# Low-part waits at the third product, and four operations moved in the order of a gated graph kernel

## The reference

```
def _L1_gnn_ref(input, in_matrix, out_matrix, ...):      # both matrices are adj
    def step(h, _):
        m_in = jnp.einsum('nm,bmd->bnd', in_matrix, h)
        m_out = jnp.einsum('nm,bmd->bnd', out_matrix, h)
        av = jnp.concatenate([m_in, m_out], axis=-1)
        u3 = h @ u3_w.T + u3_b
        z = jax.nn.sigmoid(av @ w3_w.T + w3_b + u3)
        r = jax.nn.sigmoid(av @ w4_w.T + w4_b + u3)
        hv = jnp.tanh(av @ w5_w.T + w5_b + (r * h @ u5_w.T + u5_b))
        return (1.0 - z) * h + z * hv, None
    h, _ = jax.lax.scan(step, input, None, length=5)
x = _layernorm(x + L0(x, adj))          # (adj x + x) W0 + b0, rows scaled to length 1
x = _layernorm(x + _L1_gnn_ref(x, adj, adj, ...))
x = _layernorm(x + L2(x, adj))          # D^-1/2 (adj + 1) D^-1/2 x W^T + b, D the row sums
x = _layernorm(x + L3(x, adj))          # softmax mix by a mask of adj, two weights
```

## Time and profile before

| | |
|---|---|
| median of 3 runs | 739.24 us |
| the profiled execution's own time | 740.75 us |
| its span, first to last instruction | 739.0 us |
| mean granted clock of PE | 0.995 |
| busy: PE, PE weight load, VectorE, ScalarE, GpSimd | 98%, 81%, 84%, 69%, 32% |
| slots 47 to 81, mean | 6.26 us |

### The profile page before, as it was taken

The page is one execution under the profiler, slowest core; times in us unless marked ns, Lnnn a source line. Parts: engine busy times, 40 slices in busy tenths (PEclk is TensorE's granted clock), DMA queues, the critical chain, the costliest instruction groups (busy, mean ns, idle before and its releaser), DMA issues.

```text
span 739.0 us, 11595 instructions
## 1 busy us (share of the span) xinstructions
PE 727.3 (98%) x3532; PEld 599.9 (81%) x3536; DVE 622.6 (84%) x1463; ACT 510.5 (69%) x1057; POOL 239.4 (32%) x368
## 2 busy tenths in 40 slices
PE   8999999999999989999999999999999999999996
PEld 7888787788887777777777777778888888889886
DVE  5899888999887878988888888878899999887775
ACT  4899878876666757766666666666687867863333
POOL 0878322312222312222222222220123257664433
PEclk9999999999999999999999999999999999999999
DMA  6600013334446463353333333330000000101112
GB/s 202 243 1 2 1 33 78 76 86 96 96 97 152 83 92 85 86 141 85 85 84 80 81 85 87 85 72 1 2 0 1 1 0 2 29 1 44 58 52 78
DMA packets 149661, 49.21 MB, mean 67 GB/s; under 512 B 134368, under 2 KB 135904, under 8 KB 149088
## 3 DMA queue, kind: packets, MB, share of 16 engines
q1 hardware_dynamic: 149072, 48.47, 27.2%
q10 hardware_dynamic: 528, 0.00, 0.0%
HBM read 25.11 MB, written 21.24 MB: 63 GB/s over the span
## 4 chain that ended last, share of the span: by engine, by line
PE 85%; ACT 6%; DVE 5%; DMA 3%; issue 1%; SPq 0%; POOL 0%; POOLq 0%; ACTq 0%; DVEq 0%
PE agg_ps L1161 14%; PE agg_ps L1163 13%; PE agg_ps L1162 13%; PE gate_ps L1075 7%; PE gate_ps L1077 7%; PE gate_ps L1076 7%; PE cand_ps L1075 5%; PE cand_ps L1076 4%; PE cand_ps L1077 4%; PE gate_ps L1082 3%; PE cand_ps L1082 3%; DMA state_blocks<-cand 2%; ACT feat L576 1%; PE turn_ps L1206 1%; ACT res L483 1%
## 5 line engine op out<-in xcount | busy, mean ns | idle before, releaser
L671 POOL TENSOR_TENSOR nat_lo<-nat_lo,nat_hi 128x512 fp32r<-128x512 f32 x61 | 80.5, 1320 | 293.7 <-ACT agg_hi L512 293.7
L1161 PE MATMUL agg_ps<-adj_hi,nat_hi 128*128 128x512 f32 x384 | 154.4, 402 | 0.0
L1163 PE MATMUL agg_ps<-adj_hi,nat_lo 128*128 128x512 f32 x384 | 150.4, 392 | 0.0
L1162 PE MATMUL agg_ps<-adj_lo,nat_hi 128*128 128x512 f32 x384 | 150.1, 391 | 0.0
L879 DVE TENSOR_TENSOR agg_lo<-agg_ps,agg_hi 128x512 fp32r<-128x512 f32 x80 | 55.0, 687 | 48.9 <-ACT agg_hi L512 48.9
L537 ACT ACTIVATE gate_r<-gate_ps,bias 128x512 f32<-128x512 f32 x80 | 55.2, 690 | 52.0 <-PE gate_ps L1077 52.0
L512 ACT ACTIVATE agg_hi<-agg_ps 128x512 fp32r<-128x512 f32 x80 | 48.2, 602 | 56.2 <-PE agg_ps L1163 56.2
L1163 PEld LDWEIGHTS agg_ps<-adj_hi,nat_lo 128*128 128x128 f32 x384 | 72.4, 188 | 15.9
L1162 PEld LDWEIGHTS agg_ps<-adj_lo,nat_hi 128*128 128x128 f32 x384 | 72.6, 189 | 14.2
L1161 PEld LDWEIGHTS agg_ps<-adj_hi,nat_hi 128*128 128x128 f32 x384 | 72.6, 189 | 13.8
L703 POOL TENSOR_SCALAR shift<-mean_var 128x4 f32<-128x4 f32 x62 | 24.0, 388 | 153.3 <-DVE mean_var L937 151.3
(11 more groups left out here) (207 smaller groups left out, 1751.7 us busy)
## 6 DMA issues: line engine op xcount, KB each, us to landing
state_blocks<-cand SPq DMA_DIRECT2D x61, 256.0 KB, 2.1
nat_lo<-state_blocks SPq DMA_DIRECT2D x244, 64.0 KB, 2.5
res<-in_x SPq DMA_DIRECT2D x16, 256.0 KB, 6.4
out<-res SPq DMA_DIRECT2D x16, 256.0 KB, 2.0
rows<-in_adj SPq DMA_DIRECT2D x4, 256.0 KB, 5.1
adj_hi<-eye_hi SPq DMA_DIRECT2D x1, 1024.0 KB, 9.8
adj_lo<-eye_lo SPq DMA_DIRECT2D x1, 1024.0 KB, 11.6
mix_rows<-mix SPq DMA_DIRECT2D x4, 256.0 KB, 2.8
```

Source lines behind the costliest of these rows:

```text
L671: pool.tensor_tensor(flat(nat_lo[:, u % B, :, :]), flat(nat_lo[:, u % B, :, :]).bitcast(F32), flat(nat_hi[:, u % B, :, :]).bitcast(F32), A ...
L1161: pe.matmul(ps, nat_hi[:, b, k, :], m_hi[:, k, :], start=(k == 0), stop=False)
L1162: pe.matmul(ps, nat_hi[:, b, k, :], m_lo[:, k, :], start=False, stop=False)
L1163: last = pe.matmul(ps, nat_lo[:, b, k, :], m_hi[:, k, :], start=False, stop=(k == T - 1))
```

## The change

The wait for the low part (feat_lo, agg_lo, reset_lo) moves from before a product's first matmul to before its third; the first waits for the high part. On VectorE the reset state's low part is computed before the state's add instead of after it. The row sums run one a slot in slots 40 to 43 instead of two; what follows from them moves: `WHOLE_AT` from 42 to 45, `L2_AT` from 48 to 52, row_d on GpSimd from slot 42 to 44, its transfer from slot 43 to 45, d_cols from slot 45 to 48. `SWAP_LAG` goes from 5 to 6.

```diff
--- before.py
+++ after.py
@@ -122,8 +122,8 @@
 LATE_AT = [at + 2 for at in CHOSEN_AT]
 VALUE_AT = [at + 2 for at in CHOSEN_AT]
 SUM_AT = VALUE_AT[-1] + 3
-WHOLE_AT = SUM_AT + 2
-L2_AT = WHOLE_AT + T + 2
+WHOLE_AT = SUM_AT + T + 1
+L2_AT = WHOLE_AT + T + 3
 assert L2_AT + T <= 4 * B
 
 DIAG_AT = LAST
@@ -163,7 +163,7 @@
 TURN_NO = {x: i for i, x in enumerate(TURNS)}
 
 
-SWAP_LAG = 5
+SWAP_LAG = 6
 Z_BEHIND = 0
 
 TURNED = [u for u in range(B, LAST) if u not in BY_DMA]
@@ -424,7 +424,7 @@
                     sp.wait_ge(const_made, consts)
                     sp.wait_ge(mix_stored, 16 * T)
                     sp.dma_start(diag[:, :], cells, allow_slow_non_contiguous=True).then_inc(diag_in, 16)
-                if s == SUM_AT + 5:
+                if s == WHOLE_AT + 3:
                     sp.wait_ge(d_stored, 16)
                     sp.wait_ge(turned, TURN_NO["value", T - 1] + 1)
                     sp.dma_start(d_cols[:, :], d_dram[0:1, :].to_broadcast([P, N])).then_inc(d_cols_in, 16)
@@ -595,11 +595,11 @@
                         own = slice(k * P, (k + 1) * P)
                         last = act.activation(adj_hi[:, k, own], turn_ps[n % 2][:, own], ACT.Copy)
                     last.then_inc(adj_hi_made, 1)
-                for k in range(2 * (s - SUM_AT), 2 * (s - SUM_AT) + 2):
-                    if 0 <= k < T:
-                        act.wait_ge(rows_again, 16)
-                        act.activation(chosen[:, k, :], later[:, k, :], ACT.Copy,
-                                       accum_out=row_sum[:, k:k + 1]).then_inc(row_sum_made, 1)
+                k = s - SUM_AT
+                if 0 <= k < T:
+                    act.wait_ge(rows_again, 16)
+                    act.activation(chosen[:, k, :], later[:, k, :], ACT.Copy,
+                                   accum_out=row_sum[:, k:k + 1]).then_inc(row_sum_made, 1)
                 if s in CHOSEN_AT:
                     k = CHOSEN_AT.index(s)
                     act.wait_ge(mask_made, T)
@@ -615,7 +615,7 @@
                         act.activation(w_all[:, W_L2, :], turn_ps[n % 2][:, cols:cols + D], ACT.Copy)
                     act.activation(w_hi[:, w, :], turn_ps[n % 2][:, 0:cols].rearrange("p (a d) -> p a d", d=D),
                                    ACT.Copy).then_inc(w_hi_made, 1)
-                if s == SUM_AT + 3:
+                if s == WHOLE_AT:
                     act.wait_ge(row_d_made, 1)
                     act.dma_start(d_dram[0].rearrange("(t p) -> p t", p=P), row_d[:, :],
                                  allow_slow_non_contiguous=True).then_inc(d_stored, 16)
@@ -705,7 +705,7 @@
                     pool.tensor_tensor(rstd[:, i % RING, :], r, half[:, :], ALU.pow).then_inc(rstd_made, 1)
                     pool.wait_ge(rstd_made, i + 1)
                     pool.tensor_tensor(back, back, rstd[:, i % RING, :], ALU.mult).then_inc(shift_made, 1)
-                if s == SUM_AT + 2:
+                if s == SUM_AT + T:
                     pool.wait_ge(row_sum_made, T)
                     link(pool.tensor_scalar(row_sum[:, :], row_sum[:, :], 1.0, None, ALU.add))
                     pool.tensor_tensor(row_d[:, :], row_sum[:, :], half[:, :], ALU.pow).then_inc(row_d_made, 1)
@@ -902,16 +902,16 @@
                     dve.wait_ge(feat_hi_made, s - B + 1)
                     dve.tensor_tensor(feat_lo[:, :], feat[:, s % B, :], feat_hi[:, :].bitcast(F32),
                                       ALU.subtract).then_inc(feat_lo_made, 1)
+                u = s - 1
+                if is_step(u):
+                    dve.wait_ge(reset_hi_made, u - B + 1)
+                    dve.tensor_tensor(reset_lo[:, :], gate_r[:, u % 2, :], reset_hi[:, :].bitcast(F32),
+                                      ALU.subtract).then_inc(reset_lo_made, 1)
                 u = s - 2
                 if is_step(u):
                     dve.wait_ge(move_made, u - B + 1)
                     dve.tensor_tensor(feat[:, u % B, :], feat[:, u % B, :], cand[:, u % 2, :],
                                       ALU.add).then_inc(state_made, 1)
-                u = s - 1
-                if is_step(u):
-                    dve.wait_ge(reset_hi_made, u - B + 1)
-                    dve.tensor_tensor(reset_lo[:, :], gate_r[:, u % 2, :], reset_hi[:, :].bitcast(F32),
-                                      ALU.subtract).then_inc(reset_lo_made, 1)
                 u = s - STATE_LAG
                 if is_inner(u) and u not in BY_DMA:
                     dve.wait_ge(state_hi_made, nth(TURNED, u))
@@ -1070,10 +1070,12 @@
             pe.wait_ge(eye_lo_made, T)
             first_sums(1, 2).then_inc(agg_done, 1)
 
-            def product(ps, w, hi, lo, start, stop):
+            def product(ps, w, hi, lo, start, stop, lo_made=None, count=0):
 
                 pe.matmul(ps, w_hi[:, w, :], hi, start=start, stop=False, skip_group_check=True)
                 pe.matmul(ps, w_lo[:, w, :], hi, start=False, stop=False, skip_group_check=True)
+                if lo_made is not None:
+                    pe.wait_ge(lo_made, count)
                 return pe.matmul(ps, w_hi[:, w, :], lo, start=False, stop=stop, skip_group_check=True)
 
             def by_rows(ps, m, w, stop):
@@ -1167,8 +1169,9 @@
                 u = s - 2
                 if is_step(u):
 
-                    pe.wait_ge(reset_lo_made, u - B + 1)
-                    product(cand_ps[u % 2][:, :], U_CAND, reset_hi[:, :], reset_lo[:, :], False, True).then_inc(cand_done, 1)
+                    pe.wait_ge(reset_hi_made, u - B + 1)
+                    product(cand_ps[u % 2][:, :], U_CAND, reset_hi[:, :], reset_lo[:, :], False, True,
+                            reset_lo_made, u - B + 1).then_inc(cand_done, 1)
                 u = s - 1
                 gate = gate_ps[u % 2][:, :]
                 parts = agg_hi[:, u % 2, :], agg_lo[:, u % 2, :]
@@ -1180,10 +1183,10 @@
                     if u == B:
                         pe.wait_ge(turn_read, reads(TURN_NO["weights", 1]))
 
-                    pe.wait_ge(feat_lo_made, u - B + 1)
-                    product(gate, U_GATE, feat_hi[:, :], feat_lo[:, :], True, False)
-                    pe.wait_ge(agg_lo_made, u - B + 1)
-                    product(gate, W_R, *parts, False, True).then_inc(gate_done, 1)
+                    pe.wait_ge(feat_hi_made, u - B + 1)
+                    product(gate, U_GATE, feat_hi[:, :], feat_lo[:, :], True, False, feat_lo_made, u - B + 1)
+                    pe.wait_ge(agg_hi_made, u + 1)
+                    product(gate, W_R, *parts, False, True, agg_lo_made, u - B + 1).then_inc(gate_done, 1)
                     if u >= B + 2:
                         candidate(u)
                 elif 0 <= u < UNITS:
```

## The result

The changed kernel takes 728.24 us (median of 4 runs, 728.07 to 729.18) against 739.12 us (4 runs, 737.57 to 740.31) of the kernel before: a ratio of 0.9857, 95% interval 0.9836 to 0.9877. The profiled execution's own time is 728.07 us with a span of 726.3. Forecast were 727.5 us, and 727.3 for the span. The two spans are 12.7 us apart.

The account below looks back on a forecast made before the run. PE, busy 727.3 of 739.0 us, bounds the kernel, so matmuls must come closer together. Gains of 9.1 (reset wait) and 2.6 (large stall) make 11.7, from the median of 739.24 to 727.5 us; range 725.4 to 732.2.

Parts of the forecast that it names:

- The reset wait: PE's first reset-state weight load waits for reset_lo; removing this gains 9.1 us over all slots, bounds 7.6 and 9.6.
- The second part of the loss: In ordinary slots, 0.10 us is lost at the wait and the rest of 0.14 while matmul spacing settles again.
- Slots 23 to 26: Loaded gate-step slots, two with 27 matmuls and two with 31, falling from 27.45 to 25.5 us, gain 1.9.
- The nine further slots: Slots 19, 31, 34, 37, 39, 40, 82, 89, 94: gain 0.14 us each, two some 0.15 larger, 1.5 together.
- slot 41: This slot of 7.30 us keeps its other stall and loses the reset one, gaining 0.3 us.
- both edits are needed in the loaded slots: In slot 24, reset_lo in the add's place ends at 125.26: too late for 125.08, in time for 125.53.
- a collision: VectorE's L899 took 1.80 us while GpSimd's first L671 ran; that L671 moves a slot, so this goes, within 1.9.
- The large stall: Slot 46: ScalarE's 4.45 us wait for a returned state goes, 1.1 stays; 9.90 becomes 7.3, gain 2.6, bounds 1.0 and 3.7.
- Row sums, waits between matmuls: Row sums one a slot on ScalarE: gain 0, cost 0. Waits inside PE's products, fulfilled in time: cost 0.
- The slower rival: Even fulfilled waits between a product's matmuls restart PE's stream: 240 at 0.13 us, 31 us, time 758.5; chance 0.03.
- Another product waits instead: Something else late by 0.1 us every other slot, such as gate_r; half of 9.1 stays, 732.1 us; chance 0.08.
- The trace speaks against that: Denied that a two-input VectorE add would slide under GpSimd's L671, which would cost 1.1 us.

Follow-up runs that it names:

- Experiments 1: Kernel before with only VectorE's order changed: reset_lo made ahead of the state's add; PE's waits unchanged. 732.15 us, ratio 0.9895.
- experiment 2: Kernel before with only PE's waits changed: low parts awaited before the third product, high parts before the first. 732.19 us, ratio 0.9895.
- experiment 4: Changed kernel with SWAP_LAG back at 5. 731.27 us, ratio 0.9883.
- experiments 5: Changed kernel with row sums two a slot again and everything behind them in its old slots. 728.95 us, ratio 0.985.
- experiment 6: Changed kernel with one more always fulfilled wait between first and second matmul of every gate-step product, 400 in all. 728.63 us, ratio 0.9852.
- experiments 8: Changed kernel with row_d stored as 128 packets of 16 bytes instead of 512 of 4, plus strided d_cols reads on VectorE. 727.82 us, ratio 0.9837.
- experiment 9: Changed kernel with both adj reloaded in four pieces and row_d stored in 128 packets of 16 bytes. 726.55 us, ratio 0.9803.
- experiment 10: Changed kernel with row_d in 128 packets of 16 bytes and SWAP_LAG back at 5. 727.61 us, ratio 0.9818.
- experiments 7: Changed kernel with the 1 MB reload of adj in four pieces of 256 KB, one a slot, each row sum awaiting its piece. 727.36 us, ratio 0.9832.

## Why the prediction was right, point by point

*The reset wait.* Forecast 9.1 us, found in the trace 9.0. Experiments 1 and 2 show the cause: ending reset_lo earlier, or asking for it later, gives the same 6.12. The second part of the loss was named rightly too: after a late weight load the next matmuls come at 0.23 to 0.24 instead of 0.2267, and this goes with the wait. Slots 23 to 26 gave 1.96 for 1.9, partly by luck: 6.60 and 6.16 were put for the slots with and without transposes, and they take 6.48 and 6.25 to 6.28, so the errors cancel. The nine further slots gave 1.7 for 1.5, and slot 41 less than forecast (below).

*The statement that both edits are needed in the loaded slots* holds: slots 24 and 26 are late with either one alone. The prediction also credited SWAP_LAG with taking a collision away. That is so in slot 24, but it earned nothing there beside the two edits, since experiment 4 has 6.25 as well. In slot 26 of the changed kernel a collision still stands, now with feat_lo:

```profile
134.23 1.74 POOL L671 TENSOR_TENSOR nat_lo<-nat_lo,nat_hi 128x512 fp32r<-128x512 f32 x1
134.74 1.79 DVE L903 TENSOR_TENSOR feat_lo<-feat,feat_hi 128x512 fp32r<-128x512 f32 x1
136.45 0.68 DVE L908 TENSOR_TENSOR reset_lo<-gate_r,reset_hi 128x512 fp32r<-128x512 f32 x1
```

reset_lo ends at 137.13 there, just in time for the third product, and the slot takes 6.28. The gain of slots 23 to 26 is thus that of the two edits. Either one alone beside SWAP_LAG 6 was not tried.

*The large stall.* The path was right: ScalarE no longer waits for the returned state, the tanh's wait for the outgoing one is next, and the clock holds. The size was off: 1.1 was forecast for what is left, 0.38 measured. The term that was mis-sized is the landing of the outgoing state, taken as the 7.03 of the earlier trace rows and 6.2 in the changed kernel, where row_d itself landed after 10.1 instead of 10.9. In experiments 5 and 6, where it landed after 7.5 to 7.6, this rest was 1.74 and 1.71, so a single profile's landing is good to about a microsecond, and the forecast lay in the middle. The profile of the changed kernel caught the small stall.

*Slot 41.* Forecast a gain of 0.3, measured 7.37 for 7.30, a loss of 0.07. The reset wait's share did go, but ScalarE waited 2.41 instead of 2.01 for the outgoing state. Slots 39 and 40 ahead of it had become 0.40 shorter while the transfer had not. The prediction reckoned with this in the large stall and forgot it here. This is argued from one pair of profiles, and the landing varies: with the same shorter slots slot 41 took 6.75 in experiment 2 and 7.50 in experiment 4.

*Row sums, waits between matmuls.* Both at nothing, and both were nothing (experiments 5 and 6). The slower rival, 0.13 us a wait, is excluded: 400 waits more moved no slot but the two with a DMA stall (41 and 48), which vary by as much without them.

*Another product waits instead.* Not in the changed kernel. Its neighbour, experiment 4, shows the form that it would have had. One step of the prediction fails here: "The trace speaks against that: L671 starts after agg_hi, when reset_lo or, now, the add in its place is done." This is so only while both engines are on time. In slot 26 GpSimd was late, behind its norm work, and L903 paid 1.1 us under L671 even in the changed kernel, at a cost of 0.03 to PE. In experiment 4 VectorE was late; L985 slid under L671, paid 1.0 us, and this kept VectorE late. What the Trainium skill says ("GPSIMD Engine Reference", section Specifications) on such operations contending with GpSimd was the better guide for that case, and L985's 1.26 for 0.29 and L903's 1.79 for 0.68 agree with it.

The time is 0.7 us above the forecast against the median of the kernel before, and the span 1.0 below it; the profiled run before was itself 1.5 above its median. By the medians the change gave 10.9 us, by the two profiles 12.7, and the forecast of 11.7 lies between. Of the 1.0 that the profiles show beyond it, 0.8 are the stall that was caught small and 0.3 the input transfers, less 0.1 of the reset wait, so the closeness of the total is in part luck; the path and the cost of the reset wait are not.

## What to carry to other kernels

When one engine is busy 98% and its matmuls are pipelined, measure slots from start to start and compare with a slot that has no stall; the busy share hides 0.13 us a slot, which was 1.2% here. An operand that is needed late may be asked for late, and one on the path should be made ahead of one that nobody waits for; either alone may do, and doing both gives slack for the busy slots. A buffer that is a slot later costs nothing when its reader is sixteen slots away, but ask first why the data is late: here 512 packets of 4 bytes held up transfers of 256 KB, and changing their shape took away the stall for which the extra slot had been added.

## What the runs showed of the hardware

A late weight load costs less than its own delay, but more than the gap at the wait shows: in slot 52 of the kernel before it started 0.20 us late, and PE lost 0.10 at the wait and some 0.03 more over the next eight matmuls, which came at 0.23 to 0.24 us.

512 packets of 4 bytes (2 KB) took 9.1 to 11.4 us to land and made a 256 KB write beside them take 6.2 to 7.6 for 2.1; as 128 packets of 16 bytes the same 2 KB landed in 3.2 to 3.7 us, and no state beside them was late (experiments 8 to 10).

A 256 KB write issued 2 us behind a 1 MB load took 6.4 to 7.2 us for 2.1, and slot 41 took 6.75 to 7.50 us. With the load in four pieces, one a slot, slot 41 took 6.12 (experiments 7 and 9).

A VectorE operation of 128x512 with two inputs in SBUF took 1.78 to 1.80 us for 0.68 while GpSimd's L671 ran, and L671 took 1.74 to 1.83 for 1.30.

The clock of PE fell to 1.2 GHz for 3.4 us after PE had idled 1.86 us (kernel before), 1.92 (experiment 1) and 2.08 (experiment 2), but not after 1.87 in experiment 4. What tells these apart stays open.
